# Feed-forward's second product: two 512-column products for three, and a second addition

## The reference

```
f = gelu(h @ W1 + b1) @ W2 + b2             # first stack: 256 -> 1024 -> 256, exact gelu
h = layernorm(f + h, ln2_g, ln2_b)
x = layernorm(x + h)
W1', W2' = weights composed of 32 of 64 low-rank parts each
x = layernorm(x + gelu(x @ W1') @ W2')      # second stack, tanh gelu
```

## Time and profile before

| | |
|---|---|
| median of 3 runs | 1863.13 us (1861.23 to 1863.57) |
| the profiled execution's time | 1859.66 us |
| its span, first to last instruction | 1857.9 us |
| TensorE matmuls busy | 1832.2 us, 99% |
| TensorE weight loads busy | 1528.6 us, 82% |
| VectorE busy | 1416.6 us, 76% |
| granted TensorE clock, mean | 0.998 of full |

### The profile page before, as it was taken

The page is one execution under the profiler, slowest core; times in us unless marked ns, Lnnn a source line. Parts: engine busy times, 40 slices in busy tenths (PEclk is TensorE's granted clock), DMA queues, the critical chain, the costliest instruction groups (busy, mean ns, idle before and its releaser), DMA issues.

```text
span 1857.9 us, 50038 instructions
## 1 busy us (share of the span) xinstructions
PE 1832.2 (99%) x21188; PEld 1528.6 (82%) x21188; DVE 1416.6 (76%) x3329; ACT 934.3 (50%) x1741; POOL 1011.6 (54%) x775
## 2 busy tenths in 40 slices
PE   8999999999999999999999999999999999999998
PEld 2334888888888888888887799999999999999998
DVE  3556788888888888888887767777777777777777
ACT  4554667766676667766676653232323232323231
POOL 1455999899999999899996112222222222222221
PEclk9999999999999999999999999999999999999999
DMA  8354120010102110010104940010101010101000
GB/s 291 131 207 184 56 80 17 3 36 2 36 2 104 64 56 11 2 36 2 59 2 134 308 153 32 26 44 26 44 26 44 26 44 26 44 26 42 28 12 24
DMA packets 25249, 115.62 MB, mean 62 GB/s; under 512 B 4481, under 2 KB 5441, under 8 KB 19905
## 3 DMA queue, kind: packets, MB, share of 16 engines
q1 hardware_dynamic: 21104, 89.69, 13.7%
q0 software_dynamic: 1152, 12.58, 1.9%
q10 hardware_dynamic: 2768, 10.15, 1.4%
HBM read 80.95 MB, written 31.46 MB: 61 GB/s over the span
## 4 chain that ended last, share of the span: by engine, by line
PE 96%; DVE 2%; ACT 1%; issue 0%; DMA 0%; POOL 0%; SPq 0%; ACTq 0%; DVEq 0%; POOLq 0%
PE bankC L34 13%; PE bankC L33 13%; PE bankC L32 13%; PE ring L32 7%; PE ring L34 6%; PE ring L33 6%; PE big L917 5%; PE hid_ps L241 4%; PE big L34 3%; PE big L32 3%; PE big L33 3%; PE conv_ps L253 3%; PE ring L854 3%; PE big L834 3%; PE ring L891 2%; PE ring L876 2%
## 5 line engine op out<-in xcount | busy, mean ns | idle before, releaser
L32 PE MATMUL bankC<-down_hi,act_hi 128*128 128x256 f32 x1024 | 291.4, 285 | 0.0
L34 PE MATMUL bankC<-down_hi,act_lo 128*128 128x256 f32 x1024 | 289.6, 283 | 0.0
L33 PE MATMUL bankC<-down_lo,act_hi 128*128 128x256 f32 x1024 | 288.6, 282 | 0.0
L1553 DVE TENSOR_TENSOR act_lo<-gel,act_hi 128x512 fp32r<-128x512 f32 x256 | 210.9, 824 | 8.7
L34 PE MATMUL bankC<-aT_hi,up_lo 128*128 128x512 f32 x512 | 199.7, 390 | 0.0
L33 PE MATMUL bankC<-aT_lo,up_hi 128*128 128x512 f32 x512 | 199.5, 390 | 0.0
L32 PE MATMUL bankC<-aT_hi,up_hi 128*128 128x512 f32 x512 | 199.4, 389 | 0.0
L32 PEld LDWEIGHTS bankC<-down_hi,act_hi 128*128 128x128 f32 x1024 | 193.8, 189 | 1.2
L33 PEld LDWEIGHTS bankC<-down_lo,act_hi 128*128 128x128 f32 x1024 | 193.2, 189 | 1.4
L1507 POOL TENSOR_TENSOR hC<-hC,vecC 128x1024 f32<-128x1024 f32 x16 | 38.5, 2404 | 284.5 <-PE turn L1406 284.5
L34 PEld LDWEIGHTS bankC<-down_hi,act_lo 128*128 128x128 f32 x1024 | 193.2, 189 | 0.0
(11 more groups left out here) (205 smaller groups left out, 5252.1 us busy)
## 6 DMA issues: line engine op xcount, KB each, us to landing
raw_late<-in_AB SPq DMA_DIRECT2D x30, 320.0 KB, 3.9
u<-hA SPq DMA_DIRECT2D x8, 1024.0 KB, 4.6
u_next<-u SPq DMA_DIRECT2D x8, 1024.0 KB, 4.8
hC<-u SPq DMA_DIRECT2D x16, 512.0 KB, 3.9
xC<-in_x SPq DMA_DIRECT2D x16, 512.0 KB, 4.8
out<-w_flat SPq DMA_DIRECT2D x15, 512.0 KB, 2.6
w_flat<-in_AB SPq DMA_DIRECT2D x22, 320.0 KB, 3.7
w_split<-w_parts ACTq DMA_DIRECT2D x4, 1536.0 KB, 5.3
```

The costliest lines, as they stand in the source:

```text
L32: e.matmul(out, wh, xh, start=start, stop=False)
L33: e.matmul(out, wh, xl, start=False, stop=False)
L34: return e.matmul(out, wl, xh, start=False, stop=stop)
L1553: e.tensor_tensor(a_lo[:, fb, :], g, a_hi[:, fb, :].bitcast(F32), ALU.subtract).then_inc(s_act_lo, 1)
```

## The change

The high and low parts of `down` become the two halves of one tensor `both`, 8 x 256 columns apart, so that a matmul can stream a row block of both in one instruction of 512 columns. For each `fb` and tile the three matmuls become two: act_hi by both halves (512 columns) into the whole bank, and act_lo by the high half (256 columns) into the bank's first half. For `fb` 0 the 512-column one comes first, for the others second. The bank's second half then holds act_hi by down_lo, summed over `fb`, and `evict` adds it in a second round of four additions. The first round counts a new semaphore `s_main`, the second waits for it and counts `s_y`. `last_product` and `last_tiles`, of the last phase, stay as they were.

```diff
-        down = [split("down0", [P, FB, H]), split("down1", [P, FB, H])]
+
+        both = [sb(f"down{k}", [P, 2, FB, H], F32R) for k in range(2)]
+        down = [(t[:, 0], t[:, 1]) for t in both]
...
-                        m = mm3(e, bank_of(i, k, s, FB + t)[:, 0:H], (a_hi[:, fb, tok], a_lo[:, fb, tok]),
-                                (down[k][0][:, fb, :], down[k][1][:, fb, :]), fb == 0, fb == FB - 1)
+                        bank = bank_of(i, k, s, FB + t)
+                        if fb:
+                            e.matmul(bank[:, 0:H], a_lo[:, fb, tok], both[k][:, 0, fb, :], start=False, stop=False)
+                        m = e.matmul(bank[:, :], a_hi[:, fb, tok], both[k][:, :, fb, :], start=fb == 0, stop=fb == FB - 1)
+                        if fb == 0:
+                            e.matmul(bank[:, 0:H], a_lo[:, fb, tok], both[k][:, 0, fb, :], start=False, stop=False)
...
-                    e.tensor_tensor(y[s][:, t, :], bank_of(i, k, s, FB + t)[:, 0:H], add[:, t, :], ALU.add).then_inc(s_y, 1)
+                    e.tensor_tensor(y[s][:, t, :], bank_of(i, k, s, FB + t)[:, 0:H], add[:, t, :], ALU.add).then_inc(s_main, 1)
+                for t in range(TILES):
+                    w.wait_ge(s_main, tile_no(i, k, s, t) + 1)
+                    e.tensor_tensor(y[s][:, t, :], bank_of(i, k, s, FB + t)[:, H:2 * H], y[s][:, t, :], ALU.add).then_inc(s_y, 1)
```

More of the change, by code:

```diff
@@ L1326, in ffn_phase @@
         s_up, s_gelu, s_act_hi, s_act_lo = sem("up"), sem("gelu"), sem("act_hi"), sem("act_lo")
-        s_down, s_y, s_stats, s_mom, s_var, s_rstd = (sem(n) for n in ("down", "y", "stats", "mom", "var", "rstd"))
+        s_down, s_main, s_y, s_stats, s_mom, s_var, s_rstd = (sem(n) for n in ("down", "main", "y", "stats", "mom", "var", "rstd"))
         s_centred, s_ln0, s_sum = sem("centred"), sem("ln0"), sem("sum")
```

## The result

The changed kernel takes 1875.1 us (median of 4 runs, 1873.7 to 1876.13), the kernel before 1863.1 us (median of 4). The ratio is 1.0064, 95% interval 1.0052 to 1.0077: slower by 12 us. The forecast was 8.6 us slower, 1871.7 us in a range of 1865 to 1880.

The account below looks back on a forecast made before the run. TensorE's issue pace was taken to bound the kernel; 8 x (0.93 + 0.80) us of waiting phases less 15 x 0.35 saved gave +8.6 us, 1871.7 us from the 1863.13 median, range 1865 to 1880.

Parts of the forecast that it names:

- The wait that takes over: Transposes in mid-down-product wait for apply in (0,1) and (1,0), slack 0.43 and 0.56 us: phases +0.93 and +0.80 us.
- The shift of 1.34 us: Four new additions in VectorE's evict delay all its next work by 4 x 0.335 = 1.34 us per changed phase.
- The wait on s_main: VectorE's second additions wait on this semaphore; claimed to cost nothing, as affine and centre both take 1.67 us.
- The restart: TensorE's first matmul after waiting for a VectorE result, here at the transposes: 0.15 us extra.
- The saving per tile: Down product: two matmuls instead of three take 0.3467 instead of 0.3575 us, saving 0.011 us a tile, 0.35 a phase.
- the forecast's own formula: Whole change in us: 15.9 - 0.672 s, s being ns saved per down-product tile; sign changes at s = 24.
- Rival 1: Each down-product tile's three weight loads bind it, so s = 33 ns and -6.3 us, 1856.8; chance 0.08.
- rival 2: Down product's split read costs as much as it saves, or TensorE otherwise gains nothing: +15.9 us, 1879.0; chance 0.10.
- (3): VectorE's shift never reaches the transposes, so all 31 changed phases gain: -10.8 us, 1852.3; chance 0.05.
- (4): New additions in evict don't overlap (1.66 instead of 1.34 us), or another longer restart: +5.1 us, 1876.8; chance 0.07.
- (a): Next up product's wait for a freed bank, needed 2.7 us after the down product's end, freed about 1.0: covered.
- (b): Down product's wait for pieces of act: piece 2 in (0,1) ready at 12.3 us, wanted at 13.7: covered.

Follow-up runs that it names:

- Additions alone: Kernel before, old three matmuls per tile, plus a second round of four additions in evict repeating the first: 1877.81 us against 1864.21, ratio 1.0065.
- products alone: Changed kernel without the second round of additions, so the output lacks act_hi by down_lo: 1857.54 us against 1864.21 for the kernel before, ratio 0.9966.
- the later turn: Changed kernel with the transposes one block later (TURN_AT 5 for 4): 1858.15 us against 1864.21 for the kernel before, ratio 0.9961.
- half dose: Changed kernel with two of the four second additions (tiles 0 and 1), waiting for all four of the first round: 1866.82 us, one run.

## Why the prediction was right

- **The wait that takes over: right in place, near in size.** Sixteen waits at the transposes for apply, no other in the stage. In (0,1) it was 1.02 us, where 1.28 was forecast: the transposes began 0.10 us earlier, and TensorE came 0.16 us later, since it saved less on the way. Apply ended 18.91 us into (0,1), worked out as 17.57 + 1.34 = 18.91. Additions alone, products alone and the later turn each came out as this chain says.
- **The shift of 1.34 us: right.** 1.33 us measured. The wait on s_main costs nothing tile by tile; waiting for all four at once cost 0.1 us in the half dose.
- **The restart: 0.15 us forecast, 0.05 + 0.06 measured.** The transposes began 0.05 us after apply and took 0.85 instead of 0.79 us. The forecast took it from a matmul of another kind. Over 16 phases that is 0.6 us too much.
- **The saving per tile: the term of the sum that was mis-sized.** 0.011 us forecast, 0.006 measured. The step that was off is "I take 0.011, since 512-column products here show the same remainder over the columns": it carried the up product's 0.2275 us over to the down product, where a 512-column matmul takes 0.2315. So a tile took 0.3515 us and not 0.347, and (1,1) and (0,0) 23.01 and not 22.8 to 22.9. With 6 ns the forecast's own formula gives 15.9 - 0.672 x 6 = +11.9 us, less 0.6 for the restart +11.3, beside +10.8 measured in the stage; 0.5 us of that stays unassigned. The two mis-sized terms have opposite signs, and that they partly cancel is luck. The layout, the order and the neighbour's width were each tried and are not the reason. Whether it lies in the stationary operand (act instead of up) or in the moving one stays open.
- **Rival 1, weight loads bound the product: wrong.** In the first 20 tiles the loads' busy time fell from 7.10 to 6.03 us and the product's length only from 7.10 to 7.03. The Trainium skill (Perfetto Trace Analysis, Identifying the Most-Contended Engine) would have TensorE's closeness to its roofline judged by that share, beside the share of peak operations; here the loads' busy time fell by 15% and the product's length by 1%.
- **Rivals 2 to 4.** The split read costs nothing (rival 2's mechanism), though the true saving lies about midway between its 0 and the forecast's 11 ns. The shift reached the transposes (3). The additions overlap (4), and the granted clock was 1.00 over the stage's phases, waits included.
- **The covered waits (a) and (b) stayed covered:** TensorE waits for no bank and no piece of act.

## What to carry to other kernels

An engine that is idle a tenth of a phase may have no room where its work is due in the middle: what decides is the slack at the one result that the bound engine waits for (0.43 us here), not the idle time behind it (1.8 us). When a saving on the bound engine is paid with work on another, look for that due time first, and whether the waiting step can be moved behind it: one constant turned +12 us into -6. Measure a matmul's pace in the product at hand, since the same width cost 2% more with other operands.

## What the runs showed of the hardware

- TensorE's pace in this product was the same whether the 512 moving columns are one row or two blocks 8 KB apart (20 tiles in 7.03 us both ways).
- In these products 256 columns start the next matmul after 0.117 to 0.120 us in the median, 512 after 0.227 (up) or 0.232 to 0.234 us (down). The old product ran at 0.3605 us a tile in lane 0 and 0.355 in lane 1; the new at 0.3515 in both.
- A block of 32 one-column matmuls, with TensorE busy throughout by the rows, went with a fall of the granted clock to about 0.5, the lower level of 1.2 GHz, in ten of twelve profiled executions. The fall set in during the block or at its end. In the changed kernel, where the block's products start from 1089.6 to 1093.7 us:

```profile
1092.00:1096.00 4.00, 4.00 (x20) 4.00 (x20) 1.69 (x3) 0.00 (x0) 0.00 (x0) 0.51 0.17 51
1096.00:1099.00 3.00, 3.00 (x16) 3.00 (x16) 0.00 (x0) 0.00 (x0) 0.00 (x0) 0.51 0.87 274
1099.00:1103.00 4.00, 4.00 (x35) 4.00 (x35) 1.62 (x2) 2.30 (x3) 0.00 (x0) 1.00 0.94 298
```

The sixteen waits of about 1 us at the transposes did not lower it: 1.00 in the windows of both phases with a wait above.
